# A transformer block's feed-forward: both 1024x1024 layers by Strassen's scheme over pairs of token groups

## The chip, the cores and the metric

One core of a Trainium2 chip. The metric is the device time of one execution in microseconds; the kernel before has a median of 494.87 over three runs (493.62 to 496.91). Engine names: TensorE (PE, and PEld for its weight loads), VectorE (DVE), ScalarE (ACT), GpSimd (POOL), SyncE (SP).

## What is computed

Two blocks over 2048 tokens of width 256: cross attention, a mixture of 16 experts, a second attention-like addition, and a feed-forward network with ternary weights. The change is in the last:

```python
def _tlin(x, w, s):
    return jnp.einsum('bsi,oi->bso', x, w) * s
h = jax.nn.silu(_tlin(x, w1_w, w1_s)) * _tlin(x, w2_w, w2_s)   # 256 -> 1024
h = jax.nn.gelu(_tlin(h, h1_w, h1_s), approximate=False)       # 1024 -> 1024
h = jax.nn.gelu(_tlin(h, h2_w, h2_s), approximate=False)       # 1024 -> 1024
return _tlin(h, w3_w, w3_s)                                    # 1024 -> 256
```

The entries of `w1_w`, `w2_w`, `h1_w`, `h2_w` and `w3_w` are -1, 0 and 1. `x` is the residual stream after a layer norm, and the result, times tanh of a gate, is added to it.

## The kernel before

The program is written engine by engine (`@block.tensor`, `@block.vector`, `@block.scalar`, `@block.gpsimd`, `@block.sync`), each a fixed list of instructions in the order of the code; counted semaphores tie them together. Up to about 172 us attention, routing and the experts run; then comes `ffn(g, more, general)` (L1977 on TensorE, L1291 on VectorE, L1563 on ScalarE) for four groups g of 512 tokens, one after the other. Activations lie features by tokens, in chunks of 128 features by 512 tokens.

An activation is kept as two fp32r parts: `h[0]`, its rounding, and `h[1]`, what that leaves. The ternary weights are exact in fp32r, so a product needs two matmuls. Per group:

- Gate and up (L1997 to L2011): 8 output blocks m of 8 matmuls. ScalarE takes silu out of PSUM (L1573), VectorE multiplies by the other bank (L1296), ScalarE rounds (L1577), VectorE subtracts (L1300).
- Two 1024x1024 layers (L2018 to L2053): 8 output blocks of 16 matmuls with 512 columns, L2038 on the rounding and L2039 on the rest, over banks 0 to 3. ScalarE's gelu (L1587) brings a block out, VectorE casts it (L1313) and subtracts (L1315).
- The last product w3 (L2062 to L2075): 64 matmuls of 256 columns; VectorE scales (L1352, in the last group L1342), GpSimd adds the residual (`add_residual`, L700, in the last group VectorE's L1349).

Between the layers' blocks TensorE does what the next group needs first: `T3` (8 transposes, L1955), `part1` (24 matmuls), `T4` (8 transposes, L1974). For the same group VectorE has `x2` (per tile L1146, L1149, L1154, L1156), `low3`, `x3` (L1265, L755), `normalise4` (L1274) and `low4`; GpSimd has eight gathers (L640), `root` (L583) and `add_row` (L694). All weights, 44 panels of 128 x 512, stay in SBUF. VectorE compares each with a fresh copy (`check_panel`, L1288); if one is not exact, all groups are done again with three matmuls a product (the general path, which these inputs don't take).

Of the kernel before, what the change touches and what calls it, by code (L numbers as in the profile page):

```python
# [50 lines left out]
LATE = 16  # L51
# [7 lines left out]
FIRST_PAN = NRAW + (3 * 4 * 4 * 256) // (4 * 512)  # L59
DVE_PAN = 8  # L60
# [16 lines left out]
NCHK = 11  # L77
# [38 lines left out]
def flamingo_kernel(nc, x, ctxT, cols, rows, wq, wkT, wvT, gate, experts, w1T, w2T, panels, consts, identity, out):  # L116
    with ExitStack() as ctx:
# [19 lines left out]
        Wr, w_end = place("Wr", [P, NPAN * PANEL], F32R)  # L137
        w_off = w_end - 4 * NPAN * PANEL
        Wraw = nc.alloc_sbuf_tensor_at("Wraw", [P, NPAN * PANEL], F32, offset=w_off)
        Ah, _ = place("Ah", [P, 4096], F32R)  # L140
        Al, _ = place("Al", [P, 4096], F32R)
        Bh, _ = place("Bh", [P, 4096], F32R)
        bl_off = at[0]
        Bl, b_end = place("Bl", [P, 4096], F32R)
# [5 lines left out]
        sg, _ = place("sg", [P, 3, GN])  # L150
# [33 lines left out]
        def over(start, end):  # L184
# [15 lines left out]
        e_off = w_end - 4 * LATE * PANEL  # L200
# [86 lines left out]
        outb = nc.alloc_sbuf_tensor_at("outb", [P, TG, D], F32, offset=bl_off)  # L287

        hA = [Ah[:, :].rearrange("p (k t) -> p k t", k=FK), Al[:, :].rearrange("p (k t) -> p k t", k=FK)]
        hB = [Bh[:, :].rearrange("p (k t) -> p k t", k=FK), Bl[:, :].rearrange("p (k t) -> p k t", k=FK)]  # L290
# [16 lines left out]

        pe_setup, act_setup, dve_setup = sem("pe_setup"), sem("act_setup"), sem("dve_setup")
# [8 lines left out]
        dve_flag, act_pan, dve_pan = sem("dve_flag"), sem("act_pan"), sem("dve_pan")  # L317
        dve_chk = sem("dve_chk")
        dma_chk, dma_gen = [sem(f"dma_chk{b}") for b in range(2)], [sem(f"dma_gen{b}") for b in range(2)]
# [16 lines left out]
        f_pe, f_act, f_h, f_hh, f_hl = ([sem(f"{k}{s}") for s in range(FK)] for k in  # L336
                                        ("f_pe", "f_act", "f_h", "f_hh", "f_hl"))
        f_w3, f_w3r = [sem("f_w3a"), sem("f_w3b")], sem("f_w3r")
        f_out, f_dma, f_even = sem("f_out"), sem("f_dma"), sem("f_even")

        OUT_DONE = 16 + 16 * (NG - 1) + 16 * TG
# [29 lines left out]
        def load_raw(eng, w):  # L371

            if w >= 4:
                eng.wait_ge(dma_pan[w % 4], 16 * (w // 4))
            eng.dma_start(Wraw[:, w * PANEL:(w + 1) * PANEL], panels[w]).then_inc(dma_pan[w % 4], 16)
# [3 lines left out]

        def raw_there(eng, w):  # L380
            eng.wait_ge(dma_pan[w % 4], 16 * (w // 4) + 16)

        def panel(w):
            return Wr[:, w * PANEL:(w + 1) * PANEL], Wraw[:, w * PANEL:(w + 1) * PANEL]

        def counted(g):

            return g + 2
# [21 lines left out]
        def _(eng):  # L410
# [62 lines left out]
            panel_at = [PAN_AT + 3 * (w // 2) + w % 2 if w < DVE_PAN else PAN_AT + 12 + 2 * (w - DVE_PAN) for w in range(NRAW)]  # L473
# [21 lines left out]

            eng.wait_ge(b_y, NBLK)
            for n in range(NRAW, NPAN):
                if n == FIRST_PAN:

                    eng.wait_ge(f_pe[FK - 1], 1)  # L500
                load_raw(eng, n)

            def load_check(w):
                if w >= 2:
                    eng.wait_ge(dve_chk, w - 1)
                eng.dma_start(stage[:, w % 2, :], panels[w]).then_inc(dma_chk[w % 2], 16)

            def store_tiles(g, done):
                for j in range(TG):
                    eng.wait_ge(f_out, done + j + 1)  # L510
                    eng.dma_start(out_tiles[:, g * TG + j, :], outb[:, j, :]).then_inc(f_dma, 16)

            def store_halves(g, done):
                for q in range(2):
                    eng.wait_ge(f_out, done + q + 1)
                    eng.dma_start(out_tiles[:, g * TG + 2 * q:g * TG + 2 * q + 2, :],
                                  outb[:, 2 * q:2 * q + 2, :]).then_inc(f_dma, 16)

# [22 lines left out]
        def _(eng):  # L541
# [1625 lines left out]
```

## Time and profile before

| | us |
|---|---|
| median of 3 runs (lowest, highest) | 494.87 (493.62, 496.91) |
| span of the profiled execution | 514.8 |
| TensorE busy | 482.9 (94%) |
| VectorE busy | 317.2 (62%) |
| ScalarE busy | 214.0 (42%) |
| GpSimd busy | 147.2 (29%) |

The span is what the profile shows of its own execution; no other time of it is given, and it is 20 us longer than the median of the runs. A profile's page cuts the span in 40 slices of 12.9 us and gives busy shares in tenths. Windows give busy time per engine in a stretch, with the granted clock of TensorE as a share of 2.4 GHz. Group rows give the count, the busy sum, and the mean in ns of one instruction. Matmuls overlap, so the time of one is read from the distance of their starts.

### The profile page before, as it was taken

How to read it: one execution, taken by the hardware profiler on the slowest of the kernel's cores; microseconds unless marked ns; L12 is line 12 of the kernel's file. 1: busy time of each engine (PE TensorE's matmuls, PEld its weight loads, DVE VectorE, ACT ScalarE, POOL GpSimd, SP SyncE). 2: the span in 40 equal slices, each digit the busy share in tenths (PEclk: the TensorE clock that was granted, in tenths of full speed). 3: DMA queues.
4: the chain of work that ended last, by engine and by line, in shares of the span. 5: the costliest groups of instructions: out<-in, count | busy, mean ns of one | idle time of the engine just before them, and what ended most of it. 6: DMA issues, size and time to landing. Idle time of an engine off the chain costs nothing.

```text
span 514.8 us, 7849 instructions
## 1 busy us (share of the span) xinstructions
PE 482.9 (94%) x2754; PEld 414.0 (80%) x2754; DVE 317.2 (62%) x850; ACT 214.0 (42%) x444; POOL 147.2 (29%) x154
## 2 busy tenths in 40 slices
PE   8898977994889899999999999999999999999996
PEld 7787867893879678888987888897888888788886
DVE  3988855872668577548456874537677633745433
ACT  4569924671547695621254221126222133621210
POOL 1677674647562141101071110126011101000000
PEclk9989997997799999999999999999999999999999
DMA  8967432795572558422041220005032002021101
GB/s 290 339 251 245 156 93 83 211 290 167 166 220 94 177 185 268 148 81 61 22 143 43 64 78 24 1 1 163 22 102 62 1 1 81 2 77 66 42 1 47
DMA packets 34480, 58.81 MB, mean 114 GB/s; under 512 B 4545, under 2 KB 18369, under 8 KB 34370
## 3 DMA queue, kind: packets, MB, share of 16 engines
q1 hardware_dynamic: 29776, 47.12, 27.9%
q0 software_dynamic: 3840, 10.49, 7.2%
q10 hardware_dynamic: 818, 0.61, 0.4%
q8 instruction: 25, 0.41, 0.3%
q14 instruction: 21, 0.17, 0.1%
HBM read 47.85 MB, written 14.42 MB: 121 GB/s over the span
## 4 chain that ended last, share of the span: by engine, by line
PE 77%; DVE 4%; another core or an unknown queue 3%; ACT 2%; issue 2%; DMA 1%; POOLq 0%
PE bank L2038 23%; PE bank L2039 23%; PE bank L2010 6%; PE bank L2007 5%; PE bank L1613 3%; PE bank L1615 3%; PE bank L1614 3%; PE bank L2071 3%; PE bank L2070 3%; PE bank L1850 2%; PE bank L1853 1%; DVE turned L1019 1%; ACT xb L1429 1%; DMA xg_more<-xb_dram,perm 1%
## 5 line engine op out<-in xcount | busy, mean ns | idle before, releaser
L1587 ACT ACTIVATE sg<-bank,colv 128x512 f32<-128x512 f32 x64 | 44.1, 690 | 177.2 <-PE bank L2039 177.2
L2038 PE MATMUL bank<-Ah,Wr 128*128 128x512 f32 x256 | 100.3, 392 | 0.6 <-DVE sg L1296 0.6
L2038 PE MATMUL bank<-Bh,Wr 128*128 128x512 f32 x256 | 99.9, 390 | 0.0
L2039 PE MATMUL bank<-Bl,Wr 128*128 128x512 f32 x256 | 99.7, 389 | 0.0
L2039 PE MATMUL bank<-Al,Wr 128*128 128x512 f32 x256 | 99.7, 389 | 0.0
L2038 PEld LDWEIGHTS bank<-Ah,Wr 128*128 128x128 f32 x256 | 48.0, 188 | 11.9 <-DVE sg L1296 1.4
L2039 PEld LDWEIGHTS bank<-Bl,Wr 128*128 128x128 f32 x256 | 48.1, 188 | 9.8
L2038 PEld LDWEIGHTS bank<-Bh,Wr 128*128 128x128 f32 x256 | 48.1, 188 | 9.8
L2039 PEld LDWEIGHTS bank<-Al,Wr 128*128 128x128 f32 x256 | 48.1, 188 | 9.7
L1313 DVE CAST Ah<-sg 128x512 fp32r<-128x512 f32 x32 | 13.6, 426 | 60.1 <-ACT sg L1587 60.1
L1613 PE MATMUL bank<-EL,turned 128*128 (+1 forms) x133 | 42.7, 321 | 1.2 <-issue 0.9
L583 POOL TENSOR_TENSOR rstd<-veps,mhalf 128x4 f32<-128x4 f32 x6 | 8.4, 1400 | 108.8 <-DVE veps L762 61.1
L1614 PE MATMUL bank<-EH,turned 128*128 (+1 forms) x133 | 38.7, 291 | 0.0
L1615 PE MATMUL bank<-EH,turned 128*128 (+1 forms) x133 | 38.5, 290 | 0.0
L1296 DVE SCALAR_TENSOR_TENSOR sg<-bank,colv,sg 128x512 f32<-128x512 f32 x32 | 24.0, 751 | 23.1 <-ACT sg L1573 20.3
L1573 ACT ACTIVATE sg<-bank,colv 128x512 f32<-128x512 f32 x32 | 22.1, 690 | 38.4 <-PE bank L2010 35.3
L1313 DVE CAST Bh<-sg 128x512 fp32r<-128x512 f32 x32 | 13.6, 426 | 39.4 <-ACT sg L1587 39.4
L2007 PE MATMUL bank<-xTh,Wr 128*128 128x512 f32 x96 | 37.7, 392 | 0.0
L2010 PE MATMUL bank<-xTl,Wr 128*128 128x512 f32 x96 | 37.6, 392 | 0.0
L659 POOL DMA_INDIRECT xg<-xb_dram,perm x32 | 31.7, 991 | 15.5 <-PE bank L1853 6.9
L1019 DVE TENSOR_TENSOR turned<-bank,turned 128x384 fp32r<-128x384 f32 (+1 forms) x47 | 24.9, 530 | 13.6 <-ACT turned L1505 7.7
L2071 PE MATMUL bank<-Wr,Al 128*128 128x256 f32 x128 | 30.9, 283 | 0.0
(295 smaller groups left out, 1036.9 us busy)
## 6 DMA issues: line engine op xcount, KB each, us to landing
Wraw<-panels SPq DMA_DIRECT2D x44, 256.0 KB
stage<-panels SPq DMA_DIRECT2D x44, 256.0 KB
ES<-experts SPq DMA_DIRECT2D x16, 384.0 KB, 5.7
ys_dram<-yb SPq DMA_DIRECT2D x47, 128.0 KB
ys_dram<-x SPq DMA_DIRECT2D x1, 1920.0 KB, 8.8
X<-x SPq DMA_DIRECT2D x3, 512.0 KB, 7.8
xb_dram<-xb SPq DMA_DIRECT2D x3, 512.0 KB, 4.5
out<-outb SPq DMA_DIRECT2D x3, 512.0 KB
```

The source lines that it names most:

```text
L659: eng.indirect_dma_start(out=rows, out_offset=None, in_=xb_dram, in_offset=bass.IndirectOffsetOnAxis(ap=perm[:, i:i + 1], axis=0)).then_in ...
L1019: eng.tensor_tensor(low_[:, w], bank_t[b][:, w], high_[:, w].bitcast(F32), ALU.subtract).then_inc(b_xl, 1)
L1313: own(eng.tensor_copy(h[0][:, m, :], sg[:, r, :]))
L1587: eng.activation(sg[:, (8 * layer + m) % 3, :], bank[m % 4][:, :], ACT.Gelu, scale=colv[:, c + m:c + m + 1]).then_inc(f_act[m], 1)
L1613: mm(dst, lhs[0], rhs[1], start=first, stop=False)
L1614: mm(dst, lhs[1], rhs[0], start=False, stop=False)
L1615: return mm(dst, lhs[0], rhs[0], start=False, stop=last)
L2007: mm(dst, w[:, u, k, :], x_high[:, k, :], start=k == 0, stop=False)
L2010: ins = mm(dst, w[:, u, k, :], x_low[:, k, :], start=False, stop=k == DK - 1 and not general)
L2038: mm(bank[m % 4][:, :], Wr[:, base:base + P], h[0][:, k, :], start=k == 0, stop=False)
L2039: ins = mm(bank[m % 4][:, :], Wr[:, base:base + P], h[1][:, k, :], start=False, stop=k == FK - 1 and not general)
L2071: ins = mm(dst, hA[1][:, k, j * P:(j + 1) * P], w, start=False, stop=k == FK - 1)
```

## The change

Token groups are taken in pairs p: groups 2p and 2p + 1. A layer L (0 and 1 for pair 0, 2 and 3 for pair 1) is a product of a 2 x 2 block matrix of weights (512 x 512 each: A11, A12, A21, A22) with 2 x 2 blocks of activations (512 features by 512 tokens). In place of eight block products there are seven, in the order P1, P2, P6, P7, P4, P5, P3, each of 4 output blocks of 8 matmuls (L2622 on the rounding, L2626 on the rest). P1, P6, P7 and P4 add up in banks 4 to 7, P2, P5 and P3 run in banks 0 to 3.

- TensorE: per layer and pair 224 matmuls of 512 columns for 256.
- VectorE: operands `operand1` and `operand2` (L1552, L1567: differences of two activation tiles in SBUF), `split` for each of 28 chunks (L1536, operand less its rounding), `sum_out` (L1574, a bank plus a kept product). The casts L1313 are gone from it.
- ScalarE: rounds all operands (`rounded`, Copy), copies P1, P6 and P7 out to `U` and `U3` (`keep_product`), takes gelu from SBUF except for P4. It also rounds 56 panels in this phase (`weights`) and writes |w| of all 44 into the single buffer `ck`, which VectorE compares with its own sign (`check`, L1522); the check is now that a weight is 0, 1 or -1.
- GpSimd: four sums of weight blocks per layer (`sums`, L843), each in halves of 128 x 1024, and eight operand subtractions of 128 x 512 (L887, L894); beside these the gathers, roots and row additions of before.
- SyncE loads weights by blocks of 512 x 512 into six slots, a layer's after the one before it has been used. The slots don't hold both layers, so each pair loads them again; the second load is the one that half of the checks read.
- The last layer keeps its 128 matmuls a pair. T3, part1 and T4 move: T4(1) stands at the end of P2 of layer 0, T4(3) inside P1 of layer 2, T4(2) inside P4 of layer 1.
- The general path is written anew with buffers of its own; on GpSimd four single value loads stand in place of one for four values.

```diff
+P1, P2, P6, P7, P4, P5, P3 = range(7)
+STAGES = 2 * 7 + 4
...
+PLAN = {
+    "experts": whole((0, A11)), "w0": whole((0, A12)), "w1": whole((0, A21)),
+    (0, P6): whole((0, A22)), (0, P7): whole(W3_AT, 0, 2), (0, P4): whole((1, A11)),
...
+            def sums(L, i, h):
...
+                dst, l, r, op = ((4, c, d, ALU.add), (5, e, a, ALU.subtract), (2, a, c, ALU.subtract),
+                                 (0, b, f, ALU.subtract))[i]
+                eng.tensor_tensor(WS[W_SLOTS[L][dst]][:, o], l, r, op).then_inc(pool_s[i], 1)
...
+            def operand3(L, c):
+
+                _, s12, _, s22, _ = RAW_SLOTS[L]
+                eng.wait_ge(dve_t2, 4 * L + c + 1)
+                eng.tensor_tensor(R[s12][:, c, :], R[s22][:, c, :], R[s12][:, c, :], ALU.subtract).then_inc(pool_t3, 1)
...
+            def check(place, first=0, end=NPAN):
+
+                for c in PLAN.get(place, [])[first:end]:
+                    if is_checked(c):
+                        n = CHECK_ORDER.index(c)
+                        eng.wait_ge(act_ck, n + 1)
+                        eng.scalar_tensor_tensor(ck[:, :], ck[:, :], 0.0, ck[:, :], ALU.is_gt, ALU.not_equal,
+                                                 accum_out=diff[:, n:n + 1]).then_inc(dve_chk, 1)
...
+            def split(stage, src_, c):
+
+                eng.wait_ge(act_hi, 4 * stage + c + 1)
+                eng.tensor_tensor(Ol[stage % 2][:, c, :], src_(c), Oh[stage % 2][:, c, :].bitcast(F32),
+                                  ALU.subtract).then_inc(dve_lo, 1)
...
+            def sum_out(L, which, m):
+
+                q, kept, kept_q, to = ((P2, U, P1, 4), (P5, U3, P7, 2), (P3, U, P6, 0))[which]
+                eng.wait_ge(pe_m, 4 * stage_of(L, q) + m + 1)
+                eng.wait_ge(act_ev, brought(L, kept_q, m))
+                eng.tensor_tensor(R[RAW_SLOTS[L][to]][:, m, :], in_Y(m)[:, :], kept[:, m, :], ALU.add).then_inc(dve_ad, 1)
...
+            def rounded(stage, src_, c):
+
+                if c == 0 and stage >= 2:
+                    eng.wait_ge(pe_m, 4 * (stage - 2) + 4)
+                eng.activation(Oh[stage % 2][:, c, :], src_(c), ACT.Copy).then_inc(act_hi, 1)
...
+                for k in chunks:
+                    base = m * PANEL + k * P
+                    if k == chunks[0] or m == 0:
+                        eng.wait_ge(act_hi, 4 * stage + k + 1)
+                    mm(dst, w[:, base:base + P], Oh[stage % 2][:, k, :], start=q in (P1, P2, P5) and k == 0, stop=False,
+                       skip_group_check=True)
+                    if k == chunks[0] or m == 0:
+                        eng.wait_ge(dve_lo, 4 * stage + k + 1)
+                    ins = mm(dst, w[:, base:base + P], Ol[stage % 2][:, k, :], start=False, stop=k == HC - 1,
+                             skip_group_check=True)
```

VectorE before, in layer 1 of a group, at the end of the next group's row additions: from there a check, a cast and a subtraction by turns (`stage` is the fresh copy, `Bh` and `Bl` the parts of the layer's result):

```order
L1156 BN_AGGR mv<-stats 128x2
L1248 TENSOR_SCALAR veps<-mv 128x4
L1288 SCALAR_TENSOR_TENSOR stage,diff<-stage,Wr 128x512
L1313 CAST Bh<-sg 128x512
L1315 TENSOR_TENSOR Bl<-sg,Bh 128x512
```

VectorE after, in layer 1 of pair 0: the splits of P2 (`Ol` from operand `R` and its rounding `Oh`), `operand1`, three checks, then `operand2` into `tmp`, the splits of P6 and the sums of P2:

```order
L1536 TENSOR_TENSOR Ol_210<-R_214,Oh_208 128x512 x4
L1552 TENSOR_TENSOR R_217<-R_213,R_217 128x512 x4
L1522 SCALAR_TENSOR_TENSOR ck,diff<-ck 128x512 x3
L1567 TENSOR_TENSOR tmp<-R_215,R_217 128x512 x2
L1536 TENSOR_TENSOR Ol_211<-tmp,Oh_209 128x512
L1574 TENSOR_TENSOR R_216<-bank,U 128x512
```

The last three kinds go on by turns until each has been there four times. Operands, splits and checks now stand in one queue ahead of P6 of layer 1; the casts are gone.

GpSimd before, between two groups (`xn` and `y_60` take the gathered rows, two for each of four tiles):

```order
L640 DMA xn<-ys_dram,slots 128x256
L640 DMA y_60<-ys_dram,slots 128x256
L583 TENSOR_TENSOR rstd<-veps,mhalf 128x4
L694 TENSOR_TENSOR X<-X,crow 128x1024
L583 TENSOR_TENSOR rstd<-veps,mhalf 128x4
L700 TENSOR_TENSOR outb<-outb,X 128x1024
```

GpSimd after, from the end of layer 0 to the second half of layer 1 (`WS` are the weight slots, `WSraw` the same as loaded, `R` and `tmp` activations):

```order
L843 TENSOR_TENSOR WS_198<-WSraw_202,WSraw_203 128x1024 x2
L843 TENSOR_TENSOR WS_194<-WS_198,WS_195 128x1024 x2
L894 TENSOR_TENSOR R_214<-R_214,tmp 128x512 x2
L887 TENSOR_TENSOR R_213<-R_215,R_213 128x512
L894 TENSOR_TENSOR R_214<-R_214,tmp 128x512
L887 TENSOR_TENSOR R_213<-R_215,R_213 128x512
L894 TENSOR_TENSOR R_214<-R_214,tmp 128x512
L887 TENSOR_TENSOR R_213<-R_215,R_213 128x512 x2
L843 TENSOR_TENSOR WS_196<-WS_195,WSraw_202 128x1024 x2
L718 TENSOR_TENSOR rstd<-veps,mhalf 128x4
L828 TENSOR_TENSOR X<-X,crow 128x1024
L843 TENSOR_TENSOR WS_195<-WS_199,WS_194 128x1024 x2
```

The root and the row addition of before stand among sixteen new passes per layer.

## Rows read from the trace of the kernel before

**Rows 1.** The page: TensorE's sum, its 40 slices, the chain by line.
```profile
PE 482.9 (94%) x2754; PEld 414.0 (80%) x2754; DVE 317.2 (62%) x850; ACT 214.0 (42%) x444; POOL 147.2 (29%) x154
...
PE   8898977994889899999999999999999999999996
...
PE bank L2038 23%; PE bank L2039 23%; PE bank L2010 6%; PE bank L2007 5%; PE bank L1613 3%; PE bank L1615 3%; PE bank L1614 3%; PE bank L2071 3%; PE bank L2070 3%; PE bank L1850 2%; PE bank L1853 1%; DVE turned L1019 1%; ACT xb L1429 1%; DMA xg_more<-xb_dram,perm 1%
```

**Rows 2.** Windows: gate of group 0, layers of 0, w3 of 0, layer 2 of 3.
```profile
core 0: us, PE busy (x) PEld busy (x) DVE busy (x) ACT busy (x) POOL busy (x), PEclk, DMA share, GB/s
172.40:187.20 14.80, 14.78 (x64) 11.59 (x64) 10.27 (x19) 11.38 (x20) 6.26 (x6) 1.00 0.54 174
187.20:217.20 30.00, 30.00 (x137) 24.71 (x136) 19.11 (x38) 19.47 (x34) 5.93 (x4) 1.00 0.71 230
217.20:250.10 32.90, 32.90 (x162) 27.78 (x161) 20.15 (x53) 7.53 (x12) 1.39 (x1) 1.00 0.21 65
250.10:257.80 7.70, 7.70 (x65) 7.66 (x64) 3.62 (x7) 2.95 (x4) 0.00 (x0) 1.00 0.00 1
...
473.00:502.00 29.00, 29.00 (x130) 24.01 (x129) 11.74 (x26) 5.52 (x8) 0.57 (x2) 1.00 0.08 28
```

**Rows 3.** L2038 from 440 us: least, median, most ns; first and last start.
```profile
L2038 PE MATMUL bank<-Bh,Wr x64: 389/389/389, 473.2 to 501.7; 128*128 128x512 f32 x64
```

**Rows 4.** Waits from 185 us: total, times, longest.
```profile
ACT sg L1587 <- PE bank L2039: 177.2, 63, 5.8
...
DVE Ah L1313 <- ACT sg L1587: 60.1, 26, 4.8
```

**Rows 5.** Groups on VectorE from 185 us: busy, mean ns.
```profile
L1288 DVE SCALAR_TENSOR_TENSOR stage<-stage,Wr 128x512 f32<-128x512 f32 x44 | 30.1, 685 | 0.1
...
L1315 DVE TENSOR_TENSOR Al<-sg,Ah 128x512 fp32r<-128x512 f32 x32 | 22.2, 693 | 1.1
L1296 DVE SCALAR_TENSOR_TENSOR sg<-bank,colv,sg 128x512 f32<-128x512 f32 x27 | 20.3, 751 | 18.8 <-ACT sg L1573 16.2 <-issue 2.6
...
L1313 DVE CAST Ah<-sg 128x512 fp32r<-128x512 f32 x32 | 13.6, 426 | 60.1 <-ACT sg L1587 60.1
...
L1149 DVE SCALAR_TENSOR_TENSOR X<-y,wtop,X 128x256 f32<-128x256 f32 x12 | 5.8, 485 | 0.4
...
L1265 DVE SCALAR_TENSOR_TENSOR X<-bank,rstd,X 128x256 f32<-128x256 f32 x12 | 5.4, 473 | 0.0
L1154 DVE BATCH_NORM_STATS2 stats<-X 128x6 f32<-128x256 f32 x12 | 5.1, 428 | 0.4
...
L1352 DVE TENSOR_TENSOR outb<-bank,w3s 128x512 f32<-128x512 f32 x6 | 4.1, 692 | 11.1 <-PE bank L2071 11.1
...
L1274 DVE TENSOR_SCALAR xn<-X,mv,rstd 128x256 f32<-128x256 f32 x12 | 4.1, 408 | 0.0
...
L1288 DVE DVE_READ_ACCUMULATOR stage<-stage,Wr 128x1 f32 x44 | 3.6, 82 | 0.0
```

**Rows 6.** Groups on ScalarE, whole span.
```profile
L1587 ACT ACTIVATE sg<-bank,colv 128x512 f32<-128x512 f32 x64 | 44.1, 690 | 177.2 <-PE bank L2039 177.2
...
L1531 ACT ACTIVATE Wr<-Wraw 128x512 fp32r<-128x512 f32 x36 | 21.0, 623 | 0.0
```

**Rows 7.** Timelines of VectorE and GpSimd where both are at work: start, length.
```profile
299.97 2.77 DVE L1315 TENSOR_TENSOR Bl<-sg,Bh 128x512 fp32r<-128x512 f32 x1
...
299.71 2.48 POOL L694 TENSOR_TENSOR X<-X,crow 128x1024 f32<-128x1024 f32 x1 [9.16 <-PE bank L1955]
...
36.74 0.85 DVE L828 SCALAR_TENSOR_TENSOR pr<-bank,rstd,qkb 128x64 f32<-128x64 f32 x4
...
35.87 1.86 POOL L563 TENSOR_TENSOR rstd<-veps,mhalf 128x4 f32<-128x4 f32 x1
```

**Rows 8.** Groups on GpSimd, whole span.
```profile
L599 POOL TENSOR_TENSOR EL<-ES,EH 128x384 fp32r<-128x384 f32 x24 | 23.9, 1016 | 8.2 <-DVE pr L838 3.6 <-ACT EH L1382 3.6 <-DVE both L859 0.7
...
L700 POOL TENSOR_TENSOR outb<-outb,X 128x1024 f32<-128x1024 f32 x3 | 7.2, 2397 | 61.9 <-DVE outb L1352 61.9
```

**Rows 9.** Windows of the expert part around its longest gap.
```profile
124.00:128.00 4.00, 0.00 (x0) 0.00 (x0) 0.56 (x1) 0.49 (x1) 2.97 (x4) 0.50 0.36 109
...
132.00:136.00 4.00, 4.00 (x20) 4.00 (x20) 2.44 (x6) 1.15 (x3) 3.09 (x4) 0.50 0.85 230
136.00:140.00 4.00, 4.00 (x35) 3.89 (x34) 2.49 (x8) 2.59 (x9) 1.86 (x3) 0.99 0.53 184
```

More of the change, by code:

```diff
@@ L149, in flamingo_kernel @@
         sg_off = at[0]
-        sg, _ = place("sg", [P, 3, GN])
+        place("gap", [P, 3, GN])
         xn_off = at[0]
@@ L719, in _ @@
+            second_sum(1)
+            operands(1)
+            third_sum(1)
+            root(2, 3)
+            add_row(3)
+            fourth_sum(1)
+            root(3, 3)
+            first_sum(2)
+            second_sum(2)
+            add_residual(0)
+            add_residual(1)
+            operands(2)
+            third_sum(2)
+            fourth_sum(2)
+            first_sum(3)
+            second_sum(3)
+            operands(3)
+            third_sum(3)
+            fourth_sum(3)
             eng.wait_ge(dve_flag, 1)
@@ new lines, in later_products @@
+            def later_products(L):
+                g = L + 2
+                for c in range(HC):
+                    split_product(L, P7, c)
+                check((L, P6))
+                if g < NG:
+                    x2(g)
+                if L == 1:
+                    normalise4(2)
+                for c in range(HC):
+                    split_product(L, P4, c)
+                check((L, P7))
+                if g < NG:
+                    low3(g)
+                for c in range(HC):
+                    split_product(L, P5, c)
+                check((L, P4))
+                if L == NG - 1:
+                    eng.wait_ge(dve_chk, NPAN)
+                    own(eng.reduce_max(flagf[:, 0:1], diff[:, :], AX.X))
+                    own.done()
+                    eng.tensor_scalar(flagf[:, 0:1], flagf[:, 0:1], 1.0, None, ALU.min).then_inc(dve_flag, 1)
+                if g < NG:
+                    x3(g)
+                if L == 1:
+                    low4(2)
+                for c in range(HC):
+                    split_product(L, P3, c)
+                for m in range(HC):
+                    sum_out(L, 1, m)
+                check((L, P5))
+                for c in range(HC):
+                    if L % 2:
+                        split_last(L // 2, 0, c)
+                    else:
+                        split_product(L + 1, P1, c)
+                check((L, P3))
+                for m in range(HC):
+                    sum_out(L, 2, m)
@@ L2017, in ffn @@
[L2017 to L2029 removed]
+                            ins = mm(dst, w[:, u, k, :], x_low[:, k, :], start=False, stop=k == DK - 1)
```

1092 lines of the change are left out of this document (784 added, 308 removed).

## The prediction

> **What bounds the kernel now.** I read the page first. TensorE is busy 94% of the span, VectorE 62%, ScalarE 42%, GpSimd 29%, and from the fifteenth slice to the last but one TensorE's digit is 9, at a full clock; the chain that ended last gives 46% of the span to L2038 and L2039, the two 1024x1024 layers [rows 1]. The windows by stage say the same: TensorE is busy for all of each feed-forward stage [rows 2]. The waits show the other side: ScalarE waits 177.2 us for layer matmuls and VectorE 60.1 us for ScalarE [rows 4]. So the second half is bound by the count of matmuls, and the helpers have room. The change takes from the first and fills the second.
>
> **What it removes.** In a layer without other work the hi half of the matmul pairs starts from 473.2 to 501.7: 63 pairs in 28.5 us, so 0.226 us a matmul [rows 3]. Seven products for eight, 32 matmuls each, over 2 pairs and 2 layers: 4 x 32 = 128 matmuls, 29.0 us. One product stage is 32 x 0.226 = 7.25 us. Gate and up (14.8 us), w3 (7.7 us a group), and T3, part1 and T4 keep their size; T3 is some 1.0 us and part1 with T4 some 3.8, the layers' windows of 30.0 and 32.9 against 29.0 [rows 2].
>
> **What it adds, per pair of groups and layer.** VectorE: 28 splits (before 16, and 16 casts of 0.43 that go to ScalarE), 8 operand subtractions, 12 sums out of PSUM. A subtraction of two SBUF tiles is 0.69 us, a pass that reads PSUM 0.69 to 0.75, a check 0.69 + 0.08 [rows 5]. A check is new in one more way: ScalarE writes |w| into the single buffer ck and VectorE compares it, so in a row of checks each but the first waits for another Abs. No row shows this wait; between 0 (ScalarE ahead) and 0.69 (a whole ScalarE pass in series, [rows 6]) I take 0.69 with the hop. Behind the waiting check stand the splits of the next product on VectorE, and TensorE waits for these. ScalarE: 28 roundings, 12 copies out, 16 gelus, about 36 us by 0.62 and 0.69 [rows 6], and 100 weight passes spread over the phase. In its fullest place, the later products of layer 1, it has 20 roundings, 8 copies, 12 gelus, 22 weight passes and 4 turned copies, some 42 us for TensorE's 41: nearly full, but under VectorE's below, so it gets no term of its own. GpSimd: 8 operand subtractions of half the size of L700's 2.40 us, or by L599 (1.02 us for 384 columns) 1.36; I take 1.3. And 8 half weight sums of 1024 columns, 2.4 to 2.7, I take 2.45 [rows 8]: 30 us per layer, 120 us in all beside the 15 of add_row and add_residual.
>
> **The price that the diff doesn't show.** VectorE's split at 299.97 took 2.77 us for 0.69, and the others at 214.30 and 385.68 the same: each met a GpSimd addition, here one from 299.71 to 302.20, and ended 0.5 us behind it [rows 7]. A pass with one SBUF tile and one PSUM bank did not wait: L828 at 36.74 runs through the GpSimd power of 35.87 to 37.73 [rows 7]. So a VectorE pass over two SBUF tiles and a GpSimd pass over SBUF don't run side by side. Before, the feed-forward part had six such long GpSimd additions; now it has 70.
> The Trainium skill says this as a rule (SBUF — State Buffer, Who interferes with whom): a VectorE instruction with two SBUF inputs and a GpSimd instruction that reads SBUF share one read interface, and the later one blocks wholly; with at most one SBUF input there is no contention. The trace agrees, by the 2.77 us above. Taken strictly it speaks against this change: if every GpSimd sum met such a pass, the result would be the +94 us that the bounds below work out from rows.
>
> How much of GpSimd's time hits VectorE no row shows; the ends are none of it (it falls beside PSUM passes or waits) and all. Of VectorE's new time, 294 us with the check waits, 144 splits, 32 subtractions, 44 compares and 24 row additions, 163 us, read two SBUF tiles: 55%. I take 55% of GpSimd's time as blocking.
>
> **The sum, by stretches** (TensorE's need; VectorE's own work + 0.55 x GpSimd; stall = what is over). Row work of a group on VectorE is that of before: x2 6.4 us (4 x (2 x 0.49 + 0.43 + 0.18)), low3 1.4, x3 4.4, normalise 1.6, low4 1.4 [rows 5].
> - Group 0's gate up to group 1's: in the gate VectorE has 8 gated passes 6.0, 6 splits 4.2, 6 residuals 2.5, x2(1) 6.2: 18.9 against 14.8, and TensorE's banks wait for it: 4.1. T3(1) waits for the last row, 1. T4(1) now stands at the end of P2, where before it was inside layer 2: sum out, gelu, high, low is 2.4 with nothing else for TensorE. Stall 7.5. GpSimd's sums lie beside PSUM passes here.
> - Gate of group 1 and the later products of layer 0: TensorE 14.8 + 36.3 + 3.9 = 55. VectorE 17.5 (gated 6.0, operands 5.5, 4 checks 3.1, 4 splits 2.8) + 39.0 (20 splits 13.9, 8 sums 5.5, x2, low3 and x3 12.2, 6 checks 4.6, their waits 2.8) = 56.5; GpSimd 27.6 x 0.55 = 15.2. Stall 16.7.
> - P1 and P2 of layer 1: TensorE 14.5. VectorE 17.5 (8 splits, 8 operands, 4 sums, 3 checks with waits), GpSimd 15.3 x 0.55 = 8.4; P6 can start without its last chunk, -0.7. All of it stands ahead of P6, in one queue. Stall 10.7.
> - Later products of layer 1 and last layer of the pair: TensorE 41.0 + 15.4 = 56.4. VectorE 45.0 (9 checks with waits among them) + 15.6; GpSimd 24.5 x 0.55 = 13.5. Stall 17.7.
> - Pair 1 up to group 3's gate: VectorE has room, but T4(3) stands after two blocks of P1, and normalise4(3) behind two checks and two splits. Stall 3.5.
> - Gate of group 3 and later products of layer 2: TensorE 51.1; VectorE 14.4 + 33.5 = 47.9, GpSimd 25.1 x 0.55 = 13.8. Stall 10.6.
> - Layer 3: P1 and P2 14.5 against 13.8 + 8.4, less 0.7: stall 7.0; behind it VectorE has room. End: 1.
> Stalls together 74.7; less 29.0 gives +45.7 us. The span would go from 514.8 to 560.5. The page has no time of this execution beside the span; the median of the runs is 494.87, 20 us less. The stages that stall are set by VectorE, and I carry the difference over as it is: 494.9 + 45.7 = 541.
> Costed at nothing: the quads' DMAs (84 panels in the phase and ahead of it, by the code, for 88 before; each is issued a stage or more ahead of its sum, and a late one would hold P5 to P3 of its layer), the new SBUF layout, and the four single value loads on GpSimd ahead of the first gathers; the gathers hide up to a microsecond or two, and uncovered they would cost that once.
>
> **The bounds.** With a blocking share of 0 the stretches keep what is order alone: 7.5; 4.7 (gate 17.5 against 14.8, and P6's third chunk 2); 2.3; 4.2; 3.5; 2; 0; 1: 25.2, so -3.8. With a share of 1 they give 7.5 + 29.1 + 17.6 + 28.7 + 3.5 + 21.9 + 13.9 + 1 = 123, so +94. TensorE's clock: after the gap from 122.9 to 130.8 the rows grant 0.50, 1.2 GHz, through 124 to 136, and 0.99 after it [rows 9]. My stalls are many and of one to three microseconds, so I take none; each gap like that would cost some 4 us more.
>
> **Rivals.**
> 1. Faster. GpSimd's sums fall where VectorE reads PSUM or waits, because GpSimd, too, waits for VectorE's passes to end, and ScalarE's Abs runs ahead so that the check waits (9 us of the above, one part of each later stretch) are hidden. Price: 25.2 - 7.8 = 17.4 of stall, -11.6: 483. It decides where all stalls stay under 24 us, 1% ahead of the 29.0 saved: the first three full stretches hold 67 us of GpSimd's time, so with a blocking share under 0.1. For it: VectorE has 131 us of passes and waits that need no shared reading, as much as GpSimd's 135. Against it: they would have to fall on each other exactly, and the three collisions of before show that nothing steers them apart.
> 2. No change: share 0 to 0.1, check waits as costed: stall 25.2 to 32, so 491 to 498. For and against as above.
> 3. Fully blocked, with clock falls: GpSimd and VectorE take turns throughout. VectorE's work is in long runs of four splits, so a 2.4 us sum most often meets one. 494.9 + 67 (share 0.75) to 94: 562 to 589.
> 4. It doesn't do what it says: ruled out as far as the order shows, which has 128 fewer matmuls on TensorE.
>
> **Chances.** Forecast (share 0.1 to 0.75) 0.60, fully blocked 0.18, so slower 0.78; no change 0.09; faster 0.13. One percent, 5 us, is about what a measurement of this kernel tells from no change. Range: 486 to 580; for the forecast alone 500 to 562.
>
> **What would show it.** Right: in the feed-forward part TensorE's busy share falls from 100% to some 80%, with its idle time ended by VectorE's splits (L1536) and ScalarE's roundings; L1536's mean is well over 0.69, about 1.0 to 1.2, with single ones over 2.5; VectorE is over 85% busy from 190 us on; the stretch from layer 1's P1 to its P6 lasts some 25 us. Wrong: L1536 near 0.70 in the mean beside GpSimd's 70 sums (the price isn't paid), or idle time of TensorE that ends with ScalarE's roundings while VectorE waits (ScalarE is the bound), or with pool_s and pool_t3 (GpSimd itself is late). If L1536 is slow and the time still falls, my stretches have too little slack in them.

## The result, and the profile after

The kernel with the change takes 604.02 us (601.93 to 605.83, four runs); in the same comparison the kernel before takes 495.89 (493.62 to 499.54). The ratio is 1.2165, with a 95% interval of 1.211 to 1.2219: slower by 108 us. I had forecast slower, at 541, with a range up to 580. The direction held; the size was off by 63 us, beyond the range.

The page of the changed kernel: TensorE's sum, its slices and its granted clock, the engines of the chain, and the groups that matter.

```profile
PE 483.8 (81%) x2626; PEld 405.4 (68%) x2626; DVE 442.3 (74%) x914; ACT 340.0 (57%) x672; POOL 281.9 (47%) x218
...
PE   8899899879888968596885597598965798755995
...
PEclk9999999999999878797978599989997799876999
...
PE 30%; DVE 23%; issue 16%; POOL 11%; DMA 5%; ACT 5%; SPq 0%; DVEq 0%; ACTq 0%; POOLq 0%
...
L1536 DVE TENSOR_TENSOR Ol<-R,Oh 128x512 fp32r<-128x512 f32 x128 | 125.7, 1036 | 43.5 <-ACT Oh L1992 43.5
...
L1522 DVE SCALAR_TENSOR_TENSOR ck<-ck 128x512 f32<-128x512 f32 x44 | 46.0, 1046 | 22.5 <-ACT ck L1954 22.5
...
L843 POOL TENSOR_TENSOR WS<-WS,WS 128x1024 fp32r<-128x1024 f32 x16 | 42.0, 2646 | 17.2 <-ACT WS L1956 13.2
```

The row of nines of [rows 1] is gone. TensorE has 128 matmuls fewer (2626 for 2754) and the same busy sum (483.8 for 482.9): so a matmul takes longer in the mean, and the clock's row shows one reason, down to 5 tenths in one slice. The chain, 46% of which was the two layers' matmuls, now passes through VectorE, GpSimd and "issue". The split L1536 has 1036 ns in the mean where the same kind of pass had 693 in [rows 5], the compare L1522 has 1046 for 685.

The split between idle time and slow matmuls is read from windows over the feed-forward part alone. The first line is of the kernel before, from its first gate matmul (172.4 us) to the end:

```profile
172.40:514.80 342.40, 337.02 (x1656) 282.59 (x1656) 196.71 (x416) 114.09 (x178) 48.87 (x38) 1.00 0.23 72
```

and this of the kernel after, whose first gate matmul comes at 152.6. The first columns are the stretch, its length, and TensorE's busy time with the number of its matmuls; VectorE's follows as the third pair, and the clock stands third from the end. The other two are the middle of the part, and the chunk from the start of layer 1's P6 to the start of its P4:

```profile
152.60:600.40 447.80, 348.30 (x1528) 281.92 (x1528) 324.01 (x480) 236.88 (x407) 182.91 (x102) 0.89 0.16 53
190.00:500.00 310.00, 239.65 (x1014) 193.22 (x1013) 225.52 (x331) 171.42 (x295) 128.08 (x70) 0.87 0.17 58
...
296.30:342.20 45.90, 26.71 (x97) 20.60 (x97) 39.63 (x55) 22.85 (x42) 24.40 (x13) 0.75 0.20 69
```

The part went from 342.4 to 447.8, +105.4. Its three terms: the matmuls removed are worth 29.0 and leave 308.0 of the 337.0 busy; the 1528 that stay take 348.3, 40.3 more; and TensorE is idle for 99.5 where it was idle for 5.4, 94.1 more. −29.0 + 40.3 + 94.1 = +105.4, of the 108 measured. The 20 us by which the profiled execution of before exceeded its median lie ahead of this part (172.4 against 152.6 at its start), so nothing of them belongs here.

Where TensorE stops for long, one chain of waits holds it. The timeline of the kernel after around the gap from 459.07 to 469.76, between P6 and P7 of layer 2 (start, length, engine, line; in brackets the idle time before, and what ended it):

```profile
451.61 9.04 DVE L1536 TENSOR_TENSOR Ol<-R,Oh 128x512 fp32r<-128x512 f32 x4
...
454.48 5.63 POOL L843 TENSOR_TENSOR WS<-WS,WSraw 128x1024 fp32r<-128x1024 f32 x2
...
455.61 0.62 ACT L1956 ACTIVATE WS<-WSraw 128x512 fp32r<-128x512 f32 x1
...
458.68 0.39 PE L2626 MATMUL bank<-Ol,WS 128*128 128x512 f32 x1
460.07 5.54 POOL L843 TENSOR_TENSOR WS<-WS,WS 128x1024 fp32r<-128x1024 f32 x2
460.58 2.82 DVE L1522 SCALAR_TENSOR_TENSOR ck<-ck 128x512 f32<-128x512 f32 x1
...
463.53 0.63 ACT L1954 ACTIVATE ck<-WSraw 128x512 f32<-128x512 f32 x1 [7.30 <-DVE ck L1522]
464.06 0.61 ACT L1956 ACTIVATE WS<-WSraw 128x512 fp32r<-128x512 f32 x1
464.19 1.97 DVE L1522 SCALAR_TENSOR_TENSOR ck<-ck 128x512 f32<-128x512 f32 x1 [0.78 <-ACT ck L1954]
...
469.09 2.04 ACT L2026 ACTIVATE U<-bank 128x512 f32<-128x512 f32 x4
...
469.76 0.76 PE L2622 MATMUL bank<-Oh,WS 128*128 128x512 f32 x1 [10.70 <-issue]
```

Read it from the top. GpSimd's passes stretch VectorE's four splits to 9.04 us; the next two sums stretch the two compares behind them to 2.82 and 1.97. ScalarE has written one |w| and has the next to write (L1954), but the buffer `ck` is one, so it stands 7.3 us until the first compare is done. Behind it in ScalarE's queue stand two more |w|, each behind a compare of its own, and at last `keep_product` (L2026), which copies P6 out of banks 4 to 7. P7 adds into these banks, so TensorE stands still for 10.7 us ("issue": the profile names no releaser, the copy that begins 0.7 us ahead is one; the weight sum that P7 needs ended at 460.11, so it is not that). ScalarE is busy for 4.0 us of it. Four gaps come of such a row of checks: 10.7 and 12.6 us at this place of layers 2 and 3, 6.8 and 11.9 us in layers 0 and 1, where `part1` waits for `low3` behind ScalarE's `high` in the same queue. They are 42 of the 99.5 us.

### The profile page after: what moved, and what is told of

Read it like the earlier page. It is cut to its first block, busy times and chain, and to the rows that moved or that the text cites. A ratio compares the mean times of both kernels' runs of the same rounds, so it can differ in the third digit from the quotient of the medians.

```text
span 600.4 us, 8161 instructions
## 1 busy us (share of the span) xinstructions
PE 483.8 (81%) x2626; PEld 405.4 (68%) x2626; DVE 442.3 (74%) x914; ACT 340.0 (57%) x672; POOL 281.9 (47%) x218
## 3 DMA queue, kind: packets, MB, share of 16 engines
q1 hardware_dynamic: 28384, 46.07, 22.5%
## 4 chain that ended last, share of the span: by engine, by line
PE 30%; DVE 23%; issue 16%; POOL 11%; DMA 5%; ACT 5%; SPq 0%; DVEq 0%; ACTq 0%; POOLq 0%
DVE Ol L1536 11%; PE bank L2622 8%; PE bank L2626 8%; DVE ck L1522 4%; PE bank L2569 2%; POOL R L894 2%; POOL xg L794 2%; PE bank L2572 2%; PE bank L2182 2%; POOL R L887 2%; POOL WS L843 2%; PE bank L2184 2%; PE bank L2183 2%; DMA xg<-xb_dram,perm 1%; PE bank L2708 1%
## 5 line engine op out<-in xcount | busy, mean ns | idle before, releaser
L2622 PE MATMUL bank<-Oh,WS 128*128 128x512 f32 x448 | 187.0, 417 | 27.5 <-issue 23.3
L2626 PE MATMUL bank<-Ol,WS 128*128 128x512 f32 x448 | 188.3, 420 | 23.0 <-DVE Ol L1536 22.9
L1536 DVE TENSOR_TENSOR Ol<-R,Oh 128x512 fp32r<-128x512 f32 x128 | 125.7, 1036 | 43.5 <-ACT Oh L1992 43.5
L2622 PEld LDWEIGHTS bank<-Oh,WS 128*128 128x128 f32 x448 | 92.0, 205 | 48.3 <-issue 26.6
L2626 PEld LDWEIGHTS bank<-Ol,WS 128*128 128x128 f32 x448 | 91.6, 204 | 48.8 <-DVE Ol L1536 29.4
L1992 ACT ACTIVATE Oh<-R 128x512 fp32r<-128x512 f32 x128 | 71.6, 626 | 10.8 <-POOL R L887 7.6
L894 POOL TENSOR_TENSOR R<-R,tmp 128x512 f32<-128x512 f32 x16 | 26.6, 1666 | 77.4 <-DVE tmp L1567 77.4
L1522 DVE SCALAR_TENSOR_TENSOR ck<-ck 128x512 f32<-128x512 f32 x44 | 46.0, 1046 | 22.5 <-ACT ck L1954 22.5
L843 POOL TENSOR_TENSOR WS<-WS,WS 128x1024 fp32r<-128x1024 f32 x16 | 42.0, 2646 | 17.2 <-ACT WS L1956 13.2
L1954 ACT ACTIVATE ck<-WSraw 128x512 f32<-128x512 f32 x32 | 20.0, 626 | 40.3 <-DVE ck L1522 40.3
L2569 PE MATMUL bank<-xTh,W 128*128 128x512 f32 x96 | 39.8, 415 | 3.6 <-DVE xTl L1513 2.9
L1574 DVE TENSOR_TENSOR R<-bank,U 128x512 f32<-128x512 f32 x48 | 31.2, 682 | 15.0 <-PE bank L2626 15.0
L843 POOL TENSOR_TENSOR WS<-WSraw,WSraw 128x1024 fp32r<-128x1024 f32 x8 | 20.4, 2570 | 40.3 <-PE bank L2626 40.3
L2572 PE MATMUL bank<-xTl,W 128*128 128x512 f32 x96 | 39.1, 407 | 0.0
```

The costliest lines, as they stand in the source:

```text
L843: eng.tensor_tensor(WS[W_SLOTS[L][dst]][:, o], l, r, op).then_inc(pool_s[i], 1)
L1522: eng.scalar_tensor_tensor(ck[:, :], ck[:, :], 0.0, ck[:, :], ALU.is_gt, ALU.not_equal, accum_out=diff[:, n:n + 1]).then_inc(dve_chk, 1)
L1536: eng.tensor_tensor(Ol[stage % 2][:, c, :], src_(c), Oh[stage % 2][:, c, :].bitcast(F32), ALU.subtract).then_inc(dve_lo, 1)
L1992: eng.activation(Oh[stage % 2][:, c, :], src_(c), ACT.Copy).then_inc(act_hi, 1)
L2569: mm(dst, w[:, u, k, :], x_high[:, k, :], start=k == 0, stop=False)
L2572: ins = mm(dst, w[:, u, k, :], x_low[:, k, :], start=False, stop=k == DK - 1)
```

## The experiments

Twelve kernels, each timed beside the kernel before. Two theories at the start. A: VectorE's passes are blocked by GpSimd's reads of SBUF, as the prediction says, and that is the loss. B: the loss is the single check buffer, which couples ScalarE to VectorE.

**1. Sums as writes.** GpSimd's weight sums write a constant into the same tiles at the same places (the sums are left out).

```diff
-                eng.tensor_tensor(WS[W_SLOTS[L][dst]][:, o], l, r, op).then_inc(pool_s[i], 1)
+                eng.memset(WS[W_SLOTS[L][dst]][:, o].bitcast(F32), 1.0).then_inc(pool_s[i], 1)
```

> GpSimd's 32 half weight sums are replaced by plain writes of the same tiles (the seven products are then taken with weights that are not the sums). Theory A (GpSimd's reading passes block VectorE directly): 84 of the 153 us of reading passes go, so VectorE's excess over undisturbed lengths falls from 81 us to some 35 to 40, the split's mean from 1.05 to some 0.85 us, and the time from 602 to some 545 to 560. Theory B (the single check buffer ties ScalarE's queue to VectorE's, and this makes the long gaps): the coupling stays, and with shorter splits in front of it the four gaps of 7 to 13 us shrink but don't go; 575 to 590. If writes block VectorE as reads do: as long as they last, so a time in proportion to their length.

549.31 us, ratio 1.1034 [1.0813, 1.1254]: 54.7 less than the change as it is. The splits' mean falls from 1036 to 753 ns, the compares' from 1046 to 728, and VectorE's excess over its undisturbed lengths from 81 us to 31, more than expected. The sums are about half of the loss. The edit also shortens GpSimd's own passes (0.95 us for some 2.6), but in the kernel after I find no stop that ended with a sum: ahead of the two long ones for which the profile would allow it, the sum was done at least 9 us earlier.

**2. No checks.** ScalarE's |w| passes, VectorE's compares and their waits left out (the test of the weights is left out; the same in experiments 3 and 7).

```diff
-                        eng.activation(ck[:, :], src_, ACT.Abs).then_inc(act_ck, 1)
...
-                        eng.scalar_tensor_tensor(ck[:, :], ck[:, :], 0.0, ck[:, :], ALU.is_gt, ALU.not_equal,
-                                                 accum_out=diff[:, n:n + 1]).then_inc(dve_chk, 1)
```

> The 44 checks are left out (ScalarE's Abs and VectorE's compare), GpSimd's passes stay. Theory A: VectorE gets back the checks' own 46 us and their waits of 22 us, but its splits still meet GpSimd's sums: some 30 us less, about 570. Theory B: ScalarE's copies out of PSUM no longer stand behind a compare; the four gaps (42 us together) and the low clock behind them (some 15 us) go: 540 to 550, and the longest gap of TensorE is under 5 us.

545.89, ratio 1.0965 [1.0741, 1.1189]: 58.1 less. The splits stay blocked, and more so (mean 1133). The longest gap of TensorE is now 6 us. Theory B's part is as large as that of the sums.

**3. Both.** Experiments 1 and 2 together.

> Both of the above together. If A and B are separate costs, the gains add: some 500 to 510. If they are one chain (a blocked split in front of a check in front of a copy), the gains overlap, and this is less than 15 us below the better of the two.

506.34, ratio 1.017 [0.9947, 1.0394]: 97.7 less, 87% of 54.7 + 58.1. The two losses are nearly separate. Against the kernel before the interval leaves open whether this run is slower.

**4. Copies ahead of checks.** Nothing left out. On ScalarE `weights((L, P6))` moves behind `keep_product` of P6, `weights((L, P7))` behind that of P7; on VectorE each check moves one product later.

```diff
-                weights((L, P6))
                 for m in range(HC):
                     keep_product(L, P6, m)
                 for c in range(HC):
                     round_product(L, P4, c)
+                weights((L, P6))
```

> Nothing is left out; in the later products ScalarE's copies of P6 and P7 come ahead of its weight passes, and VectorE's checks move behind the next splits. Theory B: the four long gaps go and the clock with them, 555 to 570. Theory A alone: no GpSimd read and no VectorE pass less, so within 10 us of 602.

583.16, ratio 1.1714 [1.148, 1.1947]: 20.9 less, between the two expectations. ScalarE's longest wait for a compare falls from 15.5 to 7.7 us, TensorE's longest gap from 12.6 to 8.4. TensorE's waits for the splits rise instead (22.9 to 31.0 us): with ScalarE out of the way, VectorE is late.

**5. Operands on VectorE.** The eight operand subtractions per layer move from GpSimd to VectorE.

```diff
             def operands(L):
+                return
...
                 eng.tensor_tensor(tmp[:, c % 2, :], R[s22][:, c, :], R[s11][:, c, :], ALU.subtract).then_inc(dve_t2, 1)
+                eng.tensor_tensor(R[s21][:, c, :], R[s21][:, c, :], tmp[:, c % 2, :], ALU.subtract).then_inc(pool_t4, 1)
+                eng.tensor_tensor(R[s12][:, c, :], R[s22][:, c, :], R[s12][:, c, :], ALU.subtract).then_inc(pool_t3, 1)
```

> Nothing is left out; the 32 operand subtractions go from GpSimd to VectorE, right behind the one that makes tmp. Theory A: 53 us of GpSimd's reads go and 22 us of VectorE's own work come (0.69 each); the splits of P6, of 1.55 us in the mean, fall to 0.70, the gaps of 2.7 us ahead of P6's second and third chunk go (eight of them). Time 20 to 35 us less, 568 to 582. If GpSimd's short passes were harmless: VectorE's 22 us more, so 610 to 625.

580.91 (575.98 and 585.83; two runs, no interval): 18 to 28 less, so one of the two lies inside the expected range. 32 passes more on VectorE cost less than 32 on GpSimd that block it.

**6. No reads.** Experiment 1, and the operand passes cut to 8 columns (their values are left out as well). Checks stay.

```diff
-                eng.tensor_tensor(R[s12][:, c, :], R[s22][:, c, :], R[s12][:, c, :], ALU.subtract).then_inc(pool_t3, 1)
+                eng.tensor_tensor(R[s12][:, c, 0:8], R[s22][:, c, 0:8], R[s12][:, c, 0:8], ALU.subtract).then_inc(pool_t3, 1)
```

> The weight sums are plain writes and the operand subtractions on GpSimd cover 8 of 512 columns (the result is then not the product's). With checks. Theory A: the split's mean is 0.69 to 0.72 and VectorE's compares 0.69; against the run with writes alone 30 us less, 515 to 525. What is left over the kernel before is then the order of the work and the check waits.

528.95, ratio 1.0657 [1.0508, 1.0805], a little above what was expected. Its feed-forward window:

```profile
151.90:527.80 375.90, 330.19 (x1528) 269.79 (x1528) 251.93 (x480) 235.94 (x407) 88.18 (x102) 0.94 0.19 63
```

Nearly all of the blocking is out of it (the splits' mean is 719), and 45.7 us of idle time and 22.2 us over the 308.0 busy are left. One long gap is still there, 9.6 us ahead of `part1` in layer 1, behind checks. This is the case "blocking share 0" of the prediction, which had it at −3.8 us. It is +33.

**7. No reads, no checks.** Experiments 6 and 2.

> As the run before, and the checks left out. This is seven products for eight with the copies, roundings, splits and sums that ScalarE and VectorE need, and nothing on the shared port. 29 us of matmuls less than the kernel before and the order's stalls (25 us by my own bounds, less what belongs to checks, so some 15): 475 to 487. If it is not under 490, the scheme's own order costs more than it saves, whatever GpSimd does.

485.78, ratio 0.9787 [0.964, 0.9934], as expected: the scheme with nothing beside it gains 10 us, by the interval 3 to 18. The kernel before still makes its checks, so this is no like for like.

```profile
153.30:485.30 332.00, 314.40 (x1528) 261.05 (x1528) 218.07 (x392) 211.67 (x363) 90.48 (x102) 0.99 0.21 71
```

The same 1528 matmuls at a clock of 0.99 take 314.4, against 348.3 in the kernel after, 33.9 less. The trace of the kernel after gives the clock's part more directly: 65.9 us of TensorE's busy time lie where 0.50 is granted. There a matmul starts every 0.427 us for 0.226, so some 31 of the 40.3 us are the clock (an estimate from these rows). The other 9 were not taken apart; the end of a matmul that nothing overlaps, at each of 37 stops, would be some 6 of them (37 x (0.389 − 0.226), an estimate too).

**8. Two check buffers.** `ck` as two 16-bit halves, so that |w| may run one ahead. The entries −1, 0 and 1 are exact in 16 bits, but a weight that only rounds to one of them would now pass, so the check is weaker.

```diff
-        tmp, ck = put("tmp", [P, 2, GN]), put("ck", [P, PANEL])
+        tmp, ck = put("tmp", [P, 2, GN]), put("ck", [P, 2, PANEL], BF16)
...
-                        if n:
-                            eng.wait_ge(dve_chk, n)
+                        if n > 1:
+                            eng.wait_ge(dve_chk, n - 1)
```

> The check buffer is two buffers of half the width in bytes (16 bit), so ScalarE can be one pass ahead; all passes of both engines stay (the check then sees weights rounded to 16 bit). Theory B in its narrow form (the single buffer is the chain): the long gaps go, 560 to 575. If it is not the buffer but the place of ScalarE's weight passes ahead of its copies while VectorE's compare stands behind blocked splits: 590 to 600, with gaps over 7 us still there.

591.56, ratio 1.1918 [1.1752, 1.2085]: 12 less. VectorE's wait for |w| falls from 22.5 to 4.6 us, but ScalarE still waits 36.2 us for compares, and gaps of 11.0 and 10.2 us stay. Not the buffer is the trouble but what stands in order behind it: a second buffer moves the stop by one panel, and four stand in the row of layers 2 and 3.

**9 and 10. The check in halves.** In 9 ScalarE's |w| passes stay and the compares go; in 10 the compares stay, without a wait for ScalarE, and the |w| passes go.

```diff
 9: ScalarE
-                            eng.wait_ge(dve_chk, n)
+                            eng.wait_ge(act_ck, n)
10: VectorE
-                        eng.wait_ge(act_ck, n + 1)
```

> The checks are halved: ScalarE still writes |w| of all 44 panels into the buffer, VectorE's compare and every wait for it are left out (so the test of the weights is left out). Known: with whole checks 604, with none 546. Theory Q (the checks cost by the coupling: ScalarE's queue stands behind a compare that stands behind blocked splits): ScalarE's pass itself is nearly free, 545 to 556. Rival W (ScalarE is short of time in the later products, so 44 passes of 0.7 us count): 565 to 590.

> The other half: VectorE compares the buffer 44 times without waiting for ScalarE, whose |w| passes are left out (the buffer is set to 0 once, so the test of the weights is left out). Theory Q: only VectorE's own 44 passes of 0.8 to 1.1 us are left, in stretches where VectorE is over 85% busy about half of them count: 560 to 580. If the sum of this run's and the other half's costs is well under 58 us, the rest is the wait between the two engines. Rival V (the compare's own time is all that counts, the coupling nothing): 590 to 604.

553.65, ratio 1.1148 [1.1088, 1.1208], and 577.59, ratio 1.1647 [1.1594, 1.17]. Against the 545.89 without checks, |w| alone costs 7.8 and the compare alone 31.7; together they cost 58.1, so 18.6 are left for the wait between the two engines. That is by subtraction; the run without checks has two runs and an interval of some 11 us to either side, so the three parts are no firmer than that. Both of theory Q's ranges held. The compares' 31.7 are near what the prediction charged for them (44 x 0.77 = 33.9), but they are busy for 54.6 us here, 1241 ns in the mean, so this nearness proves little.

**11. No reads, new order.** Experiment 6 in the order of experiment 4.

> GpSimd's sums write a constant and its operand passes have 8 columns (those values are left out), checks stay, and ScalarE's copies and VectorE's checks stand in the new order of the run with copies ahead of checks. Known: old order 529, without checks 486. Theory Q: with nothing blocked most of the 43 us that the checks still cost is order, so 500 to 515. Rival: it is the checks' own work on two engines, 520 to 529.

520.8, ratio 1.0517 [1.0473, 1.0561]: 8.2 less than experiment 6, where I had expected 14 to 29. Once nothing is blocked, order is worth little and the checks' own passes most: the rival held.

**12. Three mended.** Experiments 4, 5 and 8 together, nothing left out.

> Nothing left out: copies ahead of checks (alone -21), operand passes on VectorE (alone -23) and two 16-bit check buffers (alone -12) together. If the three shorten different gaps, 548 to 562, the clock's return included; if they shorten the same long gaps, 570 to 583. No theory has it at or under 510: GpSimd's sums still block, which was worth 55.

566.33, ratio 1.1478 [1.1386, 1.157]: 37.7 less, of the 51 to 61 that the three gave one by one; between "different gaps" and "the same". It is the best kernel here that computes the whole result, with the weaker check, and 70 us slower than before. Nothing that I tried and that keeps the whole result comes near the kernel before.

The windows over each kernel's feed-forward part in one table. "Over 308.0" is TensorE's busy time less the 337.0 − 29.0 that these matmuls would take as before:

| | median | part | idle | busy over 308.0 | clock |
|---|---|---|---|---|---|
| before | 495.9 | 342.4 | 5.4 | (337.0) | 1.00 |
| 7 no reads, no checks | 485.8 | 332.0 | 17.6 | 6.4 | 0.99 |
| 3 writes, no checks | 506.3 | 348.5 | 30.5 | 10.0 | 0.97 |
| 6 no reads | 529.0 | 375.9 | 45.7 | 22.2 | 0.94 |
| 2 no checks | 545.9 | 391.3 | 53.5 | 29.8 | 0.93 |
| 1 sums as writes | 549.3 | 398.0 | 63.0 | 27.0 | 0.92 |
| 12 three mended | 566.3 | 408.5 | 68.8 | 31.7 | 0.92 |
| after | 604.0 | 447.8 | 99.5 | 40.3 | 0.89 |

## Why the prediction was right in direction and wrong in size

**What held: the price of the shared reads.** The prediction said that a VectorE pass over two SBUF tiles and a GpSimd pass over SBUF don't run side by side, and took 55% of GpSimd's time as blocking. In the kernel after, VectorE's groups in the feed-forward part exceed their undisturbed lengths by 81 us; the groups behind it:

```profile
L1536 DVE TENSOR_TENSOR Ol<-tmp,Oh 128x512 fp32r<-128x512 f32 x16 | 24.4, 1547 | 1.2 <-ACT Oh L1992 1.1
...
L1567 DVE TENSOR_TENSOR tmp<-R,R 128x512 f32<-128x512 f32 x16 | 14.1, 894 | 0.8
L1552 DVE TENSOR_TENSOR R<-R,R 128x512 f32<-128x512 f32 x16 | 10.5, 687 | 0.3
L1507 DVE TENSOR_SCALAR xn<-X,mv,rstd 128x256 f32<-128x256 f32 x12 | 8.3, 752 | 0.3 <-issue 0.3
```

That is 128 x 0.346 + 44 x 0.361 + 16 x 0.857 + 16 x 0.204 + 12 x 0.344 = 44.3 + 15.9 + 13.7 + 3.3 + 4.1 = 81.3, with 0.69, 0.685 and 0.408 as the undisturbed lengths [rows 5]. GpSimd's passes over SBUF in the same part are 152.7 us (42.0 + 21.7 + 20.4 of L843, 26.6 + 26.5 of L894 and L887, 7.9 + 7.6 of the rows), so the share is 0.53, and 0.55 was forecast. No row of before measured that share, so its nearness is in part luck. That the reads are the cause is shown pass by pass: each of the 48 splits and compares over 0.85 us overlaps a GpSimd `tensor_tensor`. L1552, which falls where GpSimd has no such pass, has 687: the same operation, undisturbed. The rule of the Trainium skill that the prediction cited beside it (SBUF — State Buffer, Who interferes with whom) says the same, and the trace agrees: the stage of `tmp` splits runs at 1.55 us for 0.69, and passes that read PSUM kept their length (L1574 682 ns). In idle time of TensorE the reads cost 99.5 − 45.7 = 53.8 us, against the forecast's 74.7 − 25.2 = 49.5.

**The step that failed: the clock.** "My stalls are many and of one to three microseconds, so I take none." The part has 40.3 us more of busy time than 308.0, some 31 of them the clock by the estimate above, and the prediction had nothing for either: the 40.3 are two thirds of the 60 us by which its sum (+45.7) missed the part's +105.4. Two things were wrong: that only a gap like that of [rows 9] lowers the clock, and that no stop would be longer than three microseconds. Experiment 9 shows it best. TensorE has just done P3 of layer 0 without a gap; these are its rows in P1 of layer 1 that waited (in brackets how long, and for what):

```profile
265.03 0.50 PE L2622 MATMUL bank<-Ol,WS 128*128 128x512 f32 x1 [1.61 <-DVE Ol L1533]
267.81 0.64 PE L2622 MATMUL bank<-Ol,WS 128*128 128x512 f32 x1 [2.04 <-DVE Ol L1533]
270.57 0.80 PE L2622 MATMUL bank<-Ol,WS 128*128 128x512 f32 x1 [1.70 <-DVE Ol L1533]
273.33 0.79 PE L2622 MATMUL bank<-Ol,WS 128*128 128x512 f32 x1 [1.54 <-DVE Ol L1533]
```

and its windows over them:

```profile
264.00:268.00 4.00, 0.93 (x3) 0.49 (x4) 4.00 (x3) 2.19 (x5) 4.00 (x3) 1.00 0.00 0
268.00:272.00 4.00, 2.09 (x4) 0.64 (x3) 4.00 (x2) 0.00 (x0) 4.00 (x2) 0.50 0.00 0
272.00:276.00 4.00, 2.67 (x6) 2.15 (x7) 3.67 (x5) 2.09 (x4) 0.72 (x1) 0.50 0.00 0
276.00:280.00 4.00, 4.00 (x14) 3.14 (x13) 2.98 (x5) 3.82 (x8) 0.00 (x0) 0.72 0.00 0
```

No wait is longer than 2.1 us, and the clock is granted at 0.50, 1.2 GHz, from 268 on and still for a part of 276 to 280, when TensorE is at work without a pause. Two waits, 1.61 and 2.04 us with two matmuls between them, stand ahead of the fall, and two more follow within it: they did what one gap of 8 us did before the change. In the table each microsecond of idle time goes with 0.33 to 0.56 of longer matmuls, 0.40 in the kernel after. With 0.40 the forecast's 80 us of idle (74.7 and the 5.4 of before) would have had 32 us more beside them, 573.

**The second step: what the checks hold up.** The stalls at a blocking share of 0 were put at 25.2. Experiment 6 has 45.7 − 5.4 = 40.3, and experiment 7, without checks, 12.2. So 15.1 of the 60 us are missing here, and the last 4.3 at the reads (53.8 for 49.5). The wait of a check was sized as one ScalarE pass, 0.69, and ScalarE "gets no term of its own". The wrong part was to look only at who waits in front (VectorE for |w|, 22.5 us in all) and not at who waits in return: ScalarE waits 72.5 us for compares, 15.5 at the longest, with copies that TensorE needs behind it. The waits of the kernel after:

```profile
ACT ck L1954 <- DVE ck L1522: 72.5, 26, 15.5
DVE Ol L1536 <- ACT Oh L1992: 44.6, 20, 6.3
...
PE bank L2622 <- issue: 23.3, 2, 12.6
PE bank L2626 <- DVE Ol L1536: 22.9, 11, 3.3
DVE ck L1522 <- ACT ck L1954: 22.5, 27, 1.3
```

**The stretches.** "Behind it VectorE has room" (layer 3, stall 1 to the end) was wrong in its place: the longest gap of all lies there. These rows are of the kernel after between P6 and P7 of layer 3:

```profile
530.53 11.04 DVE L1536 TENSOR_TENSOR Ol<-R,Oh 128x512 fp32r<-128x512 f32 x4 [1.32 <-ACT Oh L1992]
...
542.30 0.63 ACT L1954 ACTIVATE ck<-WSraw 128x512 f32<-128x512 f32 x1 [9.19 <-DVE ck L1522]
...
546.31 2.04 ACT L2026 ACTIVATE U<-bank 128x512 f32<-128x512 f32 x4
...
546.99 0.77 PE L2622 MATMUL bank<-Oh,WS 128*128 128x512 f32 x1 [12.60 <-issue]
```

A stretch-wise balance (VectorE's work against TensorE's) gives room there, and the queue's order takes it away: four splits, 11.04 us under GpSimd's sums, stand ahead of the compare that holds ScalarE's copy. In experiment 7 the same stage runs without a gap. On the other side, P1 and P2 of layer 1, forecast at 25 us with their stall, took 20.9 (275.4 to 296.3): there the two-engine balance was a little too dark.

**The signs named.** TensorE busy some 80% of the part: 78%. L1536's mean 1.0 to 1.2 with singles over 2.5: 1.036, longest 2.89. VectorE over 85% busy from 190 us on: 225.5 of 310, 73%, and this is the sign that told the cause: neither VectorE (73%) nor ScalarE (55%) nor GpSimd (41%) was full. They waited for each other. Rival 3, 562 to 589 with clock falls, had the right ingredients with the wrong split: the share was the forecast's 0.53, not its 0.75 to 1, and the clock and the checks' queue made up for it.

**What stays open.** How the 18.6 us of coupling divide among the four long gaps was not measured one by one, and the rest of the matmuls' 40.3 us beside the clock is an estimate. Whether a kernel with GpSimd's sums done elsewhere (weight sums made ahead of the feed-forward part, if SBUF had room) would win, was not tried; experiments 1 and 6, both slower than before with the sums' reads gone, make it likely that it would still be slower as long as the checks stand where they stand.

## What to carry to other kernels

When a change trades matmuls for element-wise passes, count first what reads SBUF on GpSimd: here 153 us of it lengthened VectorE's two-tile passes by about half as much, and without 138 us of it (experiment 6) the kernel was 75 us faster, so the 29 us saved were gone after some 55. Then charge the clock: on a TensorE that was full, each microsecond of idle time went with 0.33 to 0.56 us of longer matmuls, in the kernel after most of it the clock. And where two in-order engines hand a single buffer to and fro, look for what stands behind the one that waits, in both directions; the hand-over is cheap, and the queue behind it is not.

## What the hardware showed that was not expected

- A GpSimd pass that only writes SBUF does not block a VectorE pass over two SBUF tiles. The constant of 128 x 1024 takes 0.953 us (32 of them, 29.5 us in experiment 1), and in experiment 6 the 20 splits and compares that overlap nothing but such writes take 693 ns at most. The three over 0.85 us, up to 2.89, each met a row addition, which reads. I had not used this part of the rule; the Trainium skill (SBUF — State Buffer, Who interferes with whom) exempts a GpSimd instruction that only writes, and the trace agrees.
- Blocking lengthens GpSimd as well: L843 has 2.57 to 2.73 us in the mean for the 2.40 of [rows 8]; those that ran undisturbed keep 2.39 to 2.45, the others have up to 2.87. The operand subtractions have 1.67 where I had put 1.3, and the two of 32 that met no two-tile VectorE pass have 1.28. The prediction charged VectorE alone.
- A VectorE pass with one SBUF input was stretched too: the normalisation L1507 has 752 ns in the mean for 408 [rows 5], with a median of 406 and a longest of 2484: two of the twelve met a GpSimd pass. In experiment 6 one stood from 289.29 to 293.56, through a row addition and the two constant writes behind it, so this kind of pass waits for writes as well. The same section of the Trainium skill names `tensor_scalar` among the operations that can enter a mode on both port pairs and contend there; the trace agrees. The prediction's short form of the rule (at most one SBUF input, no contention) left this exception out and counted only passes with two inputs. It is 4 us in all.
- Short waits in a row, here 1.61 and 2.04 us, went ahead of a fall of the clock to 1.2 GHz as a long gap does (above).
